# Attention block, batch of 32: TensorE's wait for the output weight moved into slot 4 of each batch, and a value copy moved ahead of an exponential on ScalarE

## The chip, the cores and the metric

The kernel runs on one core of one Trainium2 chip. The metric is the time of one execution on the device in microseconds, of which the median of several runs is given. Profiles are of one execution; their times are microseconds from the first instruction. A core has five engines that run their own instruction queues and meet at semaphores: TensorE (PE in the rows; PEld is its weight load), VectorE (DVE), ScalarE (ACT), GpSimd (POOL) and SyncE (SP), which here issues all DMAs.

## The reference

For each of 32 batches of 256 tokens and 512 features the kernel computes a normalisation, attention with 16 heads of 32 features and an additive bias, an output projection and a residual:

```python
h = jnp.maximum(_layernorm(x, axis=-1), 0.0)
q, k, v = split_heads(h @ Wq.T), split_heads(h @ Wk.T), split_heads(h @ Wv.T)
a = jnp.einsum('bhnd,bhmd->bhnm', q, k) * D ** (-0.5) + 2 * adj
row_nonzero = jnp.any(a != 0, axis=-1, keepdims=True)
p = softmax(a) where row_nonzero, else 0
o = jnp.einsum('bhnm,bhmd->bhnd', p, v).transpose(0, 2, 1, 3).reshape(B, N, D)
return x + o @ Wo.T
```

(The bias is the sum of two encodings that are both `adj`.)

## The kernel before

Each engine has a program of its own, with a prologue for the weights, then `body` for batch 0, a hardware loop over batches 1 to 30, and `body` for batch 31. `body` runs over 16 slots, one for each head `hh`. In slot `hh` TensorE transposes the probabilities of head `hh` (`transpose_probs`, L429), computes the scores of head `hh + 3` (`scores`, L415), in even slots the weighted values of heads `hh - 2` and `hh - 1` (`values`, L450 and L451), and then the slot's jobs from the table `JOBS`. A job is a part of a projection product or a group of transposes: `h` (normalised tokens turned), `qk`, `v` (value block `n`), `o` (attention output turned), `y` (output product). An entry is (kind, block, batch offset, first and last product). The slots that matter here are

```python
    2: [("v", 2, 0, 2, 12), ("v", 3, 0, 0, 3)],
    3: [("v", 3, 0, 3, 12), ("o", 1, -1, 0, 4)],
    4: [("h", 0, 1, 0, 4), ("y", 0, -1, 0, 6)],
    5: [("y", 0, -1, 6, 9), ("h", 1, 1, 0, 4), ("y", 0, -1, 9, 12)],
```

So slot 4 of batch b turns tokens of batch b + 1 and starts the output product of batch b - 1. Batch 0 has no jobs with offset -1, batch 31 none with offset 1.

Jobs write into two banks of PSUM in turn. Before a job starts, `begin` (L334) waits until the block that was last in its bank is taken. Taking a block is two steps: ScalarE copies the high part (`take`, L601), then VectorE computes the low part from the copy (`take`, L796) and signals `taken`. For `v` these are L622 and L818, for `o` L626 (oT_hi) and L822 (oT_lo), for `h` L610 and L804. The `y` job of slot 4 uses the bank of the `o` job of slot 3 and also reads oT_hi and oT_lo. Its waits, in order: the bank (`taken["o"]`, block 1), then at L394 `taken["o"]`, block 0.

ScalarE's slot (L692 to L712) is, in this order: in odd slots a copy of finished head outputs (L637); the exponential of head `hh + 1` (L648, two instructions); `take` of the jobs that ended in the slot before (`ended_before`), which for slot 4 are value block 3 and then o block 1; the copy of the high part of head `hh`'s transposes (L659). VectorE's slot (L910 to L926) is: the shift of head `hh + 2` (L843), its `take`s, the low part of head `hh`'s transposes (L852). Each engine works its queue in the order written.

GpSimd folds shifted scores (`fold`, L1050 and L1056), divides and scales head outputs (`divide`, L1017 to L1030; its result `o` is what the `o` jobs transpose), adds the residual (L1042), and in batch 0, in slots 7, 9, 11 and 13, computes the four low parts of the output weight (`low_out_weight`, L1063), each of which raises `wo_split` by one. The output weight's parts are read by `y` products only. TensorE waits for all four once, between `body(0, ...)` and the loop (L521).

Of the kernel before, what the change touches and what calls it, by code (L numbers as in the profile page):

```python
# [60 lines left out]
def jobs_at(hh, first, last):  # L61

    return [j for j in JOBS[hh] if not (first and j[2] < 0) and not (last and j[2] > 0)]


def ended_before(hh, first, last):

    if hh:
        return [j[:3] for j in jobs_at(hh - 1, first, last)
                if j[4] == PRODUCTS[j[0]]]  # L70
    return [(kind, n, d - 1) for kind, n, d, _, end in JOBS[HEADS - 1]
            if end == PRODUCTS[kind] and not (first and d < 1)]


def attention_block(nc, x, adj, wq, wk, wv, wo_t, out):
    B, N, D = x.shape
    NT = N // P
    KT = D // P
# [20 lines left out]
    with ExitStack() as ctx:  # L99
# [6 lines left out]
        def sem(name):  # L106
            return ctx.enter_context(nc.semaphore(name))
# [75 lines left out]
        wo_high, wo_split = sem("wo_high"), sem("wo_split")  # L183
# [40 lines left out]
        def bank(kind, n, b):  # L224


            if isinstance(b, int) and (kind, n, b) in OTHER_BANK:
                return 1 - BANK[kind, n]
            if isinstance(b, int) and (kind, n, b) == ("v", 0, 0):
                return 3  # L230
            return BANK[kind, n]

        def count(kind, n, b):

            return b * PER_BATCH[kind] + (n + 1)

        def head_no(b, hh):
            return b * HEADS + hh
# [91 lines left out]
        def _(pe):  # L330
# [23 lines left out]
            def job(kind, n, d, start, stop, b):  # L354
                ps = job_ps[bank(kind, n, b + d)]
                if start == 0:
                    begin(kind, n, d, b)
                if kind == "h":
                    if n == 0 and start == 0:

                        pe.wait_ge(h_ready, b + (d + 1))
                    for k, t in [divmod(i, NT) for i in range(start, stop)]:
                        end = nc.tensor.transpose(ps[:, k * N + t * P:k * N + (t + 1) * P],  # L363
                                                  h[:, t, (2 * n + k) * P:(2 * n + k + 1) * P], ident[:, :])
                elif kind == "qk":
                    half = PRODUCTS["qk"] // 2
                    if n == 0 and start == 0:

                        pe.wait_ge(taken["h"], count("h", 0, b + d))
                    if n == 0 and start <= half // 2 < stop:  # L370

                        pe.wait_ge(taken["h"], count("h", 1, b + d))
                    for i, w in enumerate((WQ, WK)):
                        if start < (i + 1) * half and stop > i * half:
                            end = product(ps[:, i * N:(i + 1) * N],
                                          [lambda k, w=m: w[:, k, n * P:(n + 1) * P] for m in (w_hi[w], w_lo[w])],
                                          [lambda k, v=v: v[:, k, :] for v in hT], start - i * half, stop - i * half)
                elif kind == "v":
                    t, half = n % NT, n // NT
                    end = product(ps[:, 0:HALF], [lambda k, v=v: v[:, k, t * P:(t + 1) * P] for v in hT],  # L380
                                  [lambda k, w=w: w[:, k, half * HALF:(half + 1) * HALF] for w in (w_hi[WV], w_lo[WV])],
                                  start, stop)
                elif kind == "o":

                    if start == 0:
                        pe.wait_ge(o_ready, (b + d) * QUADS + 2 * (n + 1))
                    for k, t in [divmod(i, NT) for i in range(start, stop)]:
                        end = nc.tensor.transpose(ps[:, k * N + t * P:k * N + (t + 1) * P],  # L388
                                                  o[:, t, (2 * n + k) * P:(2 * n + k + 1) * P], ident[:, :])
                else:  # L390
                    half = PRODUCTS["y"] // 2
                    if n == 0 and start == 0:

                        pe.wait_ge(taken["o"], count("o", 0, b + d))  # L394
                    if n == 0 and start <= half < stop:

                        pe.wait_ge(taken["o"], count("o", 1, b + d))
                    end = product(ps[:, :], [lambda k, v=v: v[:, k, n * P:(n + 1) * P] for v in oT],
                                  [lambda k, w=w: w[:, k, :] for w in (wo_hi, wo_lo)], start, stop)
                if stop == PRODUCTS[kind]:  # L400
                    end.then_inc(ended[kind], 1)
# [116 lines left out]

            body(0, True, False)

            pe.wait_ge(wo_split, KT)  # L521
            with pe.Fori(1, B - 1) as b:
                body(b, False, False)
            body(B - 1, False, True)
# [38 lines left out]
        def _(act):  # L563
# [37 lines left out]
            def take(kind, n, b, early=False):  # L601

                ps = job_ps[bank(kind, n, b)]
                if kind == "y" and not (isinstance(b, int) and b == 0):

                    act.wait_ge(stored[n], b * 16)

                act.wait_ge(ended[kind], count(kind, n, b))
                if kind == "h":
                    nc.scalar.activation(hT_hi[:, 2 * n:2 * n + 2, :], ps[:, :].rearrange("p (k n) -> p k n", k=2),  # L610
                                         ACT.Relu).then_inc(high["h"], 1)
                elif kind == "qk":
                    nc.scalar.activation(qk_parts[:, n // 2, 1, n % 2, :], ps[:, 0:N], ACT.Copy,
                                         scale=q_scale[:, n:n + 1])
                    nc.scalar.activation(qk_parts[:, n // 2, 2, n % 2, :], ps[:, N:2 * N], ACT.Copy,
                                         scale=UNTOP).then_inc(high["qk"], 1)
                elif kind == "v":
                    t, half = n % NT, n // NT
                    if not early:

                        act.wait_ge(pv_done, head_no(b, 0) + (HH * (half + 1) - HEADS))
                    nc.scalar.activation(v_parts[:, t, half * HH:(half + 1) * HH, 0:HD],  # L622
                                         ps[:, 0:HALF].rearrange("p (h d) -> p h d", d=HD), ACT.Copy,
                                         scale=V_UNTOP).then_inc(high["v"], 1)
                elif kind == "o":
                    nc.scalar.activation(oT_hi[:, 2 * n:2 * n + 2, :], ps[:, :].rearrange("p (k n) -> p k n", k=2),  # L626
                                         ACT.Copy).then_inc(high["o"], 1)
                else:
                    nc.scalar.activation(y[:, n, :], ps[:, :], ACT.Copy).then_inc(taken["y"], 1)

            def copy_outputs(b, pair, early):

                act.wait_ge(pv_done, head_no(b, 2 * pair + 2))
                if not early:

                    act.wait_ge(o_ready, b * QUADS + (pair // 2 - 1))
                nc.scalar.activation(o_raw[pair // 2 % 2][:, pair % 2, :, :],  # L637
                                     o_ps[:, :].rearrange("p (q c) -> p q c", c=P)[:, :, 0:LOW + HD],
                                     ACT.Copy).then_inc(o_copied, 1)
# [51 lines left out]
            def body(b, first, last):  # L691
                for hh in range(HEADS):  # L692
                    if hh % 2:

                        if hh > 1:
                            copy_outputs(b, hh // 2 - 1, first and hh < 10)
                        elif not first:
                            copy_outputs(b - 1, PAIRS - 1, False)
                    if hh + 1 < HEADS:
                        exponentials(b, hh + 1, first and hh + 1 < 2)  # L700
                    elif not last:
                        exponentials(b + 1, 0, False)
                    for kind, n, d in ended_before(hh, first, last):
                        take(kind, n, b + d, first and (kind, d) in (("v", 0), ("qk", 0)))
                    if first and 6 <= hh < 6 + KT:

                        high_out_weight(hh - 6)
                    if hh == HEADS - 3 and not (first or last):
                        copy_adj(b + 1)
                    high_probs(b, hh, first and hh < 4)  # L710
                    if hh == HEADS - 3 and first:
                        copy_adj(b + 1)  # L712
# [429 lines left out]
```

## Time and profile before

| | us |
|---|---|
| median of 3 runs | 1256.52 (1256.03 to 1256.82) |
| profiled execution, its own time | 1256.6 |
| its span, first to last instruction | 1254.8 |
| mean granted TensorE clock | 0.999 |

| engine | busy, us | share of span |
|---|---|---|
| TensorE, products | 1230.2 | 98% |
| TensorE, weight loads | 1109.2 | 88% |
| VectorE | 1068.7 | 85% |
| ScalarE | 1044.2 | 83% |
| GpSimd | 897.1 | 71% |

A busy share says how much of the span has an instruction recorded. Products are pipelined and the ends of their records are modelled, so two starts that are further apart than usual can be a wait though no idle time is recorded between them. A record that follows a wait carries in brackets the idle time before it and what released it.

### The profile page before, as it was taken

What the parts mean: (1) busy time and instruction counts of PE and PEld (TensorE: products, weight loads), DVE (VectorE), ACT (ScalarE), POOL (GpSimd) and SP (SyncE); (2) the same over time, 40 slices, a digit from 0 to 9 for tenths busy, and PEclk for the clock granted to TensorE, in tenths of its full rate; (3) what the DMA queues carried; (4) which work ended last, traced back from release to release, by engine and by line L of the source; (5) the groups of instructions that cost most, each with busy time, mean ns of one, the idle gap of its engine ahead of it and who ended that gap; (6) DMA issues with size and microseconds to landing.
All of it is one profiled execution on the core that took longest, in us unless ns stands there. A gap on an engine that the chain in (4) does not pass through costs nothing.

```text
span 1254.8 us, 43748 instructions
## 1 busy us (share of the span) xinstructions
PE 1230.2 (98%) x13104; PEld 1109.2 (88%) x13104; DVE 1068.7 (85%) x3500; ACT 1044.2 (83%) x2429; POOL 897.1 (71%) x1268
## 2 busy tenths in 40 slices
PE   6989999999999999999999999999999999999997
PEld 5878989989989999889989899899899898998996
DVE  7878888888888888888888888888888888888887
ACT  5878888888888888888888888888888888888886
POOL 4767776777776777777777776777767777767765
PEclk9999999999999999999999999999999999999999
DMA  6536445465445454454554454654454554545533
GB/s 228 127 101 151 116 111 141 117 159 137 122 109 136 131 150 131 118 127 123 145 150 117 113 138 116 159 139 120 109 138 130 150 133 117 126 125 143 134 97 89
DMA packets 91861, 163.89 MB, mean 131 GB/s; under 512 B 15168, under 2 KB 24896, under 8 KB 91840
## 3 DMA queue, kind: packets, MB, share of 16 engines
q1 hardware_dynamic: 91840, 163.64, 50.2%
q8 instruction: 10, 0.16, 0.1%
q14 instruction: 11, 0.09, 0.0%
HBM read 46.14 MB, written 16.78 MB: 50 GB/s over the span
## 4 chain that ended last, share of the span: by engine, by line
PE 88%; POOL 6%; issue 3%; DVE 1%; ACT 0%; DMA 0%; POOLq 0%; DVEq 0%; ACTq 0%
PE job_ps L348 51%; PE pT_ps L429 16%; PE s_ps L415 9%; PE o_ps L450 6%; PE o_ps L451 2%; POOL fold L1050 2%; PE job_ps L363 2%; PE job_ps L388 2%; POOL bounds L1056 1%; POOL o_raw L1024 1%; POOL o L1030 0%; POOL y L1042 0%; POOL wo_lo L1063 0%; DVE minus L843 0%; POOL h L1009 0%
## 5 line engine op out<-in xcount | busy, mean ns | idle before, releaser
L1050 POOL TENSOR_TENSOR fold<-minus 128x512 f32<-128x512 f32 x256 | 326.2, 1274 | 247.5 <-DVE bounds L843 247.4
L648 ACT ACTIVATE probs<-minus,bounds 128x256 f32<-128x256 f32 x1024 | 461.7, 503 | 10.8 <-DVE bounds L843 10.7
L852 DVE TENSOR_TENSOR pT_lo<-pT_ps,pT_hi 128x512 f16<-128x512 f32 x512 | 350.3, 684 | 124.8 <-ACT pT_hi L659 124.5
L843 DVE CUSTOM_DVE_ANT_0 minus<-s_ps,adj_now 128x256 f32<-128x256 f32 x1024 | 388.8, 417 | 13.1 <-issue 6.6
L659 ACT ACTIVATE pT_hi<-pT_ps 128x512 f16<-128x512 f32 x512 | 305.8, 597 | 111.2 <-PE pT_ps L429 109.5
L429 PE MATMUL pT_ps<-ident,probs 128*128 128x128 f32 x2048 | 308.1, 273 | 4.5 <-POOL wo_lo L1063 2.8
L348 PE MATMUL job_ps<-hT_hi,w_hi 128*128 128x256 f16 x1024 | 280.7, 274 | 1.3 <-DVE hT_lo L804 1.0
L348 PE MATMUL job_ps<-hT_hi,w_lo 128*128 128x256 f16 x1024 | 279.5, 273 | 0.0
L348 PE MATMUL job_ps<-hT_lo,w_hi 128*128 128x256 f16 x1024 | 279.4, 273 | 0.0
L429 PEld LDWEIGHTS pT_ps<-ident,probs 128*128 128x128 f32 x2048 | 242.2, 141 | 22.3 <-issue 3.3
L415 PE MATMUL s_ps<-qk_stack 96*128 96x256 f32 x1024 | 246.7, 322 | 0.5 <-DMA qk_stack<-qk_parts 0.4
L1056 POOL TENSOR_TENSOR bounds<-fold 128x256 f32<-128x256 f32 x256 | 187.6, 733 | 25.1 <-POOL fold L1050 9.6
L415 PEld LDWEIGHTS s_ps<-qk_stack 96*128 96x128 f32 x1024 | 154.7, 191 | 1.0 <-DMA qk_stack<-qk_parts 0.7
L450 PE MATMUL o_ps<-v_parts,pT_hi 128*128 128x65 f16 x2048 | 152.3, 192 | 1.2 <-DVE pT_lo L852 1.0
L451 PE MATMUL o_ps<-v_parts,pT_lo 128*128 128x33 f16 x2048 | 146.2, 178 | 0.0
L348 PE MATMUL job_ps<-w_hi,hT_hi 128*128 128x256 f16 x508 | 139.5, 275 | 1.9 <-DVE qk_parts L812 0.9
L348 PE MATMUL job_ps<-w_lo,hT_hi 128*128 128x256 f16 x508 | 138.4, 272 | 0.0
L348 PE MATMUL job_ps<-w_hi,hT_lo 128*128 128x256 f16 x508 | 138.3, 272 | 0.0
L450 PEld LDWEIGHTS o_ps<-v_parts,pT_hi 128*128 128x128 f16 x2048 | 122.4, 96 | 13.1 <-DVE pT_lo L852 1.8
L451 PEld LDWEIGHTS o_ps<-v_parts,pT_lo 128*128 128x128 f16 x2048 | 125.3, 96 | 0.0
L348 PEld LDWEIGHTS job_ps<-hT_hi,w_hi 128*128 128x128 f16 x1024 | 99.8, 97 | 16.5 <-DVE hT_lo L804 1.1
L348 PEld LDWEIGHTS job_ps<-hT_hi,w_lo 128*128 128x128 f16 x1024 | 100.1, 98 | 12.0
(96 smaller groups left out, 2191.2 us busy)
## 6 DMA issues: line engine op xcount, KB each, us to landing
qk_stack<-qk_parts SPq DMA_DIRECT2D x756, 128.0 KB, 2.3
x_in<-x SPq DMA_DIRECT2D x32, 512.0 KB, 4.8
x_res<-x SPq DMA_DIRECT2D x32, 512.0 KB, 3.6
out<-y SPq DMA_DIRECT2D x64, 256.0 KB, 2.1
adj_in<-adj SPq DMA_DIRECT2D x32, 256.0 KB, 4.7
qk_stack<-qk_parts SPq DMA_DIRECT2D x24, 64.0 KB, 2.0
w_in<-wq SPq DMA_DIRECT2D x2, 512.0 KB, 5.4
w_in<-wk SPq DMA_DIRECT2D x2, 512.0 KB, 6.6
```

The lines of the kernel that those rows point to most:

```text
L348: end = nc.tensor.matmul(dst, lhs[a](k), rhs[c](k), start=i == 0, stop=i == len(terms) - 1)
L363: end = nc.tensor.transpose(ps[:, k * N + t * P:k * N + (t + 1) * P], h[:, t, (2 * n + k) * P:(2 * n + k + 1) * P], ident[:, :])
L415: end = nc.tensor.matmul(s_ps[SCORE_BANK[hh]][:, t * N:(t + 1) * N], stack[:, 0, t * P:(t + 1) * P], stack[:, 1, :], start=True, stop=True)
L429: end = nc.tensor.transpose(pT_ps[hh % 2][:, m * N + t * P:m * N + (t + 1) * P], probs[hh % 2][:, t, m * P:(m + 1) * P], ident[:, :])
L450: nc.tensor.matmul(ps[:, 0:LOW + HD], hi, v[:, 0:LOW + HD], start=m == 0, stop=False)
L451: end = nc.tensor.matmul(ps[:, 0:HD + 1], lo, v[:, 0:HD + 1], start=False, stop=m == NT - 1)
L648: end = nc.scalar.activation(probs[hh % 2][:, t, :], minus[hh // 2 % 2][:, hh % 2, t, :], ACT.Exp, bias=bounds[:, hh // 2 % 4, 2 * (hh % 2 ...
L659: nc.scalar.activation(pT_hi[hh % 4][:, :, :], pT_ps[hh % 2][:, :].rearrange("p (m n) -> p m n", m=NT), ACT.Copy).then_inc(pT_high, 1)
L843: end = nc.vector.tensor_tensor_reduce(out=minus[pair % 2][:, hh % 2, t, :], in0=s_ps[SCORE_BANK[hh]][:, t * N:(t + 1) * N], in1=adj_now[: ...
L852: nc.vector.tensor_tensor(pT_lo[hh % 4][:, :, :], pT_ps[hh % 2][:, :].rearrange("p (m n) -> p m n", m=NT), pT_hi[hh % 4][:, :, :], ALU.sub ...
L1050: nc.gpsimd.tensor_tensor(f1[:, :, :], src[:, :, 0:N // 2], src[:, :, N // 2:N], ALU.add).then_inc(folded1, 1)
L1056: nc.gpsimd.tensor_tensor(f2, f1[:, :, 0:N // 4], f1[:, :, N // 4:N // 2], ALU.add).then_inc(folded2, 1)
```

## The change

The wait of TensorE for the four parts of the output weight is taken out between batch 0 and the loop, and put into `job` ahead of the first `y` product of block 0, which stands in slot 4 of batches 1 to 31. On ScalarE, in slot 4 of every batch, the `take` of value block 3 is called ahead of the exponential of head 5 and left out of the list behind it. No operation is added or removed otherwise.

```diff
@@ def job
                 else:
                     half = PRODUCTS["y"] // 2
+                    if n == 0 and start == 0:
+
+                        pe.wait_ge(wo_split, KT)
                     if n == 0 and start == 0:
 
                         pe.wait_ge(taken["o"], count("o", 0, b + d))
@@ block.tensor
             body(0, True, False)
 
-            pe.wait_ge(wo_split, KT)
             with pe.Fori(1, B - 1) as b:
@@ block.scalar, body
+                    if hh == 4:
+
+                        take("v", 3, b, first)
                     if hh + 1 < HEADS:
                         exponentials(b, hh + 1, first and hh + 1 < 2)
                     elif not last:
                         exponentials(b + 1, 0, False)
                     for kind, n, d in ended_before(hh, first, last):
+                        if (kind, n) == ("v", 3):
+                            continue
                         take(kind, n, b + d, first and (kind, d) in (("v", 0), ("qk", 0)))
```

## Rows read from the trace of the kernel before

**Rows 1.** The page, part 1: busy time, share of the span, instructions.

```profile
PE 1230.2 (98%) x13104; PEld 1109.2 (88%) x13104; DVE 1068.7 (85%) x3500; ACT 1044.2 (83%) x2429; POOL 897.1 (71%) x1268
```

**Rows 2.** Timeline, TensorE, end of batch 0, start of batch 1: start, duration, instruction, [idle before].

```profile
67.10 0.27 PE L348 MATMUL job_ps<-w_hi,hT_lo 128*128 128x256 f16 x1
70.17 0.65 PE L429 MATMUL pT_ps<-ident,probs 128*128 128x128 f32 x4 [2.80 <-POOL wo_lo L1063]
...
76.55 0.60 PE L429 MATMUL pT_ps<-ident,probs 128*128 128x128 f32 x4
```

**Rows 3.** Timeline, TensorE, first output product of slot 4, batches 1 and 30.

```profile
82.87 0.50 PE L348 MATMUL job_ps<-wo_hi,oT_hi 128*128 128x512 f32 x1
...
1187.00 0.50 PE L348 MATMUL job_ps<-wo_hi,oT_hi 128*128 128x512 f32 x1
```

**Rows 4.** Timeline, TensorE, slots 3 to 5 of batch 2.

```profile
118.75 0.27 PE L348 MATMUL job_ps<-w_hi,hT_lo 128*128 128x256 f16 x1
118.86 0.60 PE L388 MATMUL job_ps<-ident,o 128*128 128x128 f32 x4
...
120.43 0.63 PE L363 MATMUL job_ps<-ident,h 128*128 128x128 f32 x4
120.95 0.50 PE L348 MATMUL job_ps<-wo_hi,oT_hi 128*128 128x512 f32 x1
...
123.80 0.60 PE L363 MATMUL job_ps<-ident,h 128*128 128x128 f32 x4
124.16 0.48 PE L348 MATMUL job_ps<-wo_hi,oT_hi 128*128 128x512 f32 x1
```

**Rows 5.** Timeline, GpSimd, end of batch 0 and start of batch 1.

```profile
68.57 1.26 POOL L1063 TENSOR_TENSOR wo_lo<-wo_in,wo_hi 128x512 fp32r<-128x512 f32 x1
69.79 1.27 POOL L1050 TENSOR_TENSOR fold<-minus 128x512 f32<-128x512 f32 x1
71.14 0.74 POOL L1056 TENSOR_TENSOR bounds<-fold 128x256 f32<-128x256 f32 x1
```

**Rows 6.** Table of windows: length, busy by engine, granted clock, DMA share, GB/s.

```profile
40.00:47.00 7.00, 5.50 (x70) 4.88 (x69) 7.00 (x22) 6.90 (x17) 5.18 (x8) 1.00 0.89 205
...
72.00:73.00 1.00, 1.00 (x6) 0.71 (x5) 1.00 (x6) 0.83 (x3) 0.00 (x0) 0.50 0.00 0
```

**Rows 7.** Timeline, TensorE, starts of slots 0 and 2 of batch 2.

```profile
109.96 0.60 PE L429 MATMUL pT_ps<-ident,probs 128*128 128x128 f32 x4
...
114.62 0.60 PE L429 MATMUL pT_ps<-ident,probs 128*128 128x128 f32 x4
```

**Rows 8.** Timeline, ScalarE and VectorE, slot 15 of batch 0.

```profile
64.98 0.91 ACT L648 ACTIVATE probs<-minus,bounds 128x256 f32<-128x256 f32 x2
...
64.97 0.68 DVE L852 TENSOR_TENSOR pT_lo<-pT_ps,pT_hi 128x512 f16<-128x512 f32 x1
```

**Rows 9.** Timeline, GpSimd, slots 1 to 3 of batch 2.

```profile
112.78 1.27 POOL L1050 TENSOR_TENSOR fold<-minus 128x512 f32<-128x512 f32 x1 [0.88 <-DVE bounds L843]
...
116.18 0.62 POOL L1030 TENSOR_TENSOR o<-o_raw,factor 128x256 f32<-128x256 f32 x1
```

**Rows 10.** Timeline, VectorE and TensorE, slot 4 of batch 31, the last.

```profile
1224.04 0.69 DVE L822 TENSOR_TENSOR oT_lo<-job_ps,oT_hi 128x512 fp32r<-128x512 f32 x1
...
1224.79 0.51 PE L348 MATMUL job_ps<-wo_hi,oT_hi 128*128 128x512 f32 x1 [0.29 <-DVE oT_lo L822]
```

**Rows 11.** Timeline, ScalarE, slot 4 of batch 2.

```profile
118.31 0.90 ACT L648 ACTIVATE probs<-minus,bounds 128x256 f32<-128x256 f32 x2
119.10 0.37 ACT L622 ACTIVATE v_parts<-job_ps 128x256 f16<-128x256 f32 x1
119.49 0.60 ACT L626 ACTIVATE oT_hi<-job_ps 128x512 fp32r<-128x512 f32 x1
```

**Rows 12.** Timeline, VectorE, slot 4 of batch 2.

```profile
120.12 0.69 DVE L822 TENSOR_TENSOR oT_lo<-job_ps,oT_hi 128x512 fp32r<-128x512 f32 x1
```

**Rows 13.** Timeline, TensorE, a wait in slot 6 of batch 0.

```profile
46.31 0.27 PE L348 MATMUL job_ps<-hT_hi,w_hi 128*128 128x256 f16 x1 [0.99 <-DVE hT_lo L804]
```

## The prediction

> **What bounds the kernel now.** The page comes first: TensorE is busy for 98% of the span [rows 1], so whatever moves TensorE's next instruction moves the end. Next comes the timeline of TensorE at its longest wait behind the prologue. It shows one large hole, between the last product of batch 0 and the first transpose of batch 1, ended by GpSimd's wo_lo [rows 2]. Then come the starts of one instruction over all batches: the first output product of slot 4 starts at 82.87 in batch 1 and at 1187.00 in batch 30 [rows 3], so a batch takes (1187.00 - 82.87) / 29 = 38.07 us. Anything that is added once in each batch counts 31 times. Last comes slot 4 on all engines, where the second half of the change lies; its rows are named there.
>
> **Part one: the wait for wo_split.** It stands before batch 1, though the output weight is first read in slot 4 of batch 1. TensorE's last product of batch 0 starts at 67.10, and the next instruction could start 0.11 later (the step from the last value product to the o transposes, 118.75 to 118.86, [rows 4]), at 67.21. It starts at 70.17, just after the fourth wo_lo ends at 68.57 + 1.26 = 69.83 [rows 2, 5]. That is 2.96 us. Behind the hole TensorE runs at half its clock: granted 0.50 in 72 to 73 (1.2 GHz of 2.4) [rows 6]. Slots 0 and 1 take 76.55 - 70.17 = 6.38 us in batch 1 and 114.62 - 109.96 = 4.66 in batch 2 [rows 2, 7], so the slow clock costs 1.72. Both go if nothing else is late: 4.68 us.
>
> What is late next? The first transposes of batch 1 need head 0's exponential, which ended at 64.98 + 0.91 = 65.89, and the split of head 14, which ended at 64.97 + 0.68 = 65.65 [rows 8]. Neither holds at 67.21. GpSimd is behind by its backlog: its fold of batch 1's pair 0 ends its second step at 71.14 + 0.74 = 71.88 [rows 5], whatever TensorE does. Then it folds pair 1 and divides the last quad of batch 0, which takes from 112.78 to 116.18 + 0.62 = 116.80 in batch 2 [rows 9], 4.02 us; so o would be ready at 75.90. Its reader, the o transposes of slot 3, stands at 118.86 in batch 2 [rows 4], that is 8.90 behind the batch's start, and so at 67.21 + 8.90 = 76.11. GpSimd is just in time, by 0.2 us. The moved wait itself is long met when slot 4 comes, about 10.5 us (120.43 - 109.96, [rows 4, 7]) behind the start, against 69.83.
>
> The wait is now executed in each of 31 batches. It stands behind the wait for the bank (oT_lo of the o block before) and ahead of another wait for o. Behind it are queued the six y products and all that TensorE does later. Once met it costs only its passage. The trace of before doesn't show one alone; but in the last batch the product's record starts at 1224.79, 0.06 behind the end of oT_lo at 1224.04 + 0.69 = 1224.73 [rows 10], with one met wait passed in that time. So the bound is 0 to 0.06 each, 0 to 1.9 us in all. I take 0, since part of that 0.06 must be the signal's way. The Trainium skill speaks against this (Advanced Engine Details and Errata, Miscellaneous Facts): reading a semaphore from a sequencer takes 50 to 100 ns, by which 31 reads would be an estimate of 1.6 to 3.1 us; the 0.06 of the row speaks against the upper end.
>
> **Part two: ScalarE's order in slot 4.** Now ScalarE does, in this order: exponential of head 5 (118.31), copy of value block 3 (119.10), copy of the o transposes (oT_hi, 119.49), copy of head 4's transposes [rows 11]. The last product of value block 3 starts at 118.75 and lasts 0.27, so it ends at 119.02 [rows 4]. The copy of block 3 is therefore only 0.08 late as it is. Put ahead of the exponential, it makes ScalarE stand still until 119.02 plus the signal; with 0.03 for that (118.86 + 0.60 = 119.46 to the start of oT_hi at 119.49, [rows 4, 11]) it starts at 119.05. The exponential has been ready since 118.31 and is queued behind it.
>
> A ScalarE operation starts 0.11 before the recorded end of the one before (118.31 + 0.90 = 119.21 against 119.10). So the exponential starts at 119.05 + 0.37 - 0.11 = 119.31, and oT_hi 0.79 to 0.81 later (I take 0.80), near 120.12 instead of 119.49: 0.63 us later. VectorE starts oT_lo 0.03 behind oT_hi's end (119.49 + 0.60 = 120.09, start 120.12) and ends at 120.81 [rows 11, 12]; it comes 0.63 later too, with head 4's split queued behind it.
>
> Is oT_lo on TensorE's path? The first y product starts at 120.95, 0.14 behind oT_lo's end, and 0.52 behind the first h transpose at 120.43. The same pair in slot 5, with no wait between, takes 124.16 - 123.80 = 0.36 [rows 4]. So the y product already waits up to 0.16, and there is no cover. In the last batch, without h transposes, the profile names oT_lo as its releaser outright [rows 10]. If the release takes 0.06 as there, and 0.08 of the 0.14 is something else, the shift in TensorE is 0.55; if the 0.14 stays, 0.63. I take 0.60 for 30 batches and 0.63 for the last: 18.0 + 0.6 = 18.6 us. The bounds are 30 x 0.55 + 0.63 = 17.1 and 31 x 0.63 = 19.5.
>
> Does TensorE get it back in the batch? What it waits for later (copies of h, exponentials, scores) follows TensorE's own, equally late work or keeps its distance: ScalarE's delay behind TensorE is gone once it waits for the transposes of slot 5. What the earlier copy gives, the bank for the h transposes, is worth nothing: they start right behind the head products, and VectorE's half of the value block isn't earlier, because it is queued behind the shift of head 6.
>
> Batch 0 has no y in slot 4; there the moved copy delays head 4's copy and the h copies by at most the same 0.63. I take 0.2, with 0 and 0.6 as bounds.
>
> **Sum.** -4.68 + 18.6 + 0.2 = +14.1 us on the profiled execution's 1256.6 us (span 1254.8, so 1.8 around it): 1270.7. That execution lies 0.1 above the median of 1256.52, so 1270.6. With the bounds: 1256.5 - 4.7 + 17.1 = 1268.9 at the low end; 1256.5 - 3.0 (the hole goes, the slow clock stays) + 19.5 + 0.6 + 1.9 = 1275.5 at the high one.
>
> **Rivals.**
> - Faster. VectorE's or TensorE's queue has slack I don't see, so that a later oT_lo moves no product, and only part one remains: 1256.5 - 4.7 = 1251.8. For it: in batches 1 to 30 the profile puts no idle time of TensorE down to oT_lo. Against it: 0.52 against 0.36, and the last batch. It decides if the y product could start 0.6 us after oT_lo ended without being late, and no row shows such slack.
> - Partly absorbed. Half to two thirds of the 0.63 arrives, since a later wait of TensorE in the batch shrinks by the rest: 31 x 0.3 to 0.4 = 9.3 to 12.4, so 1261 to 1264. For it, small steps like the 0.16; against it, the period of 38.07 that is full of TensorE's own work [rows 1].
> - Part one gives nothing. GpSimd's backlog takes the place of the wait: its margin is 0.2 us, and a stall there could cost up to the hole and the slow clock again. Then 1256.5 + 18.6 + 0.2 = 1275.3.
> - The clock falls in every batch, because of the new wait of some 0.75 us. A fall costs 1.72, so 1270.6 + 31 x 1.72 = 1323.9. Against it, TensorE stood idle for 0.99 us ahead of 46.31 [rows 13], and 40 to 47 has a granted clock of 1.00 [rows 6]. The Trainium skill names this behaviour (TensorE: Matmul & The Clock Gate, HAM oscillation): a kernel in which TensorE idles briefly between groups of products can make the clock swing. By that rule the time would be this rival's; the trace, with the idle time and clock just told, disagrees for single gaps of this size.
>
> **How the numbers follow.** Forecast 0.76; only part one 0.09; partly absorbed 0.05; nothing from part one 0.07; clock falls 0.03. A difference of 0.2% (2.5 us) is about what a measurement of this kernel can tell from no change. Only the first rival is faster: 0.09. Within 0.2% lies none of the cases, and I leave 0.02 for a mixture, out of the absorbed case. Slower: 0.89. The range takes the forecast with its bounds and the stall of GpSimd, and reaches down to the upper edge of the absorbed case: 1264 to 1277. Outside are only part one, most of the absorbed case, and the clock.
>
> **What would show it.** In the profile after: no hole at 67 and no stretch of half clock behind it; batch 1's slot 4 about 4.7 us earlier than now, its y product at 82.87 - 4.7 + 0.6 = 78.8; in each slot 4 the copy of block 3 with an idle time of ScalarE of about 0.65 that ends with a product of TensorE; the exponential behind it; the first y product about 1.1 behind the first h transpose instead of 0.52, with its wait put down to oT_lo; a period of 38.67 instead of 38.07. The prediction is wrong if that step stays near 0.5, if the period grows by less than 0.5, or if TensorE meets a new wait between 67 and 77.

## The result and the profile after

The changed kernel takes 1273.36 us (median of 4 runs, 1272.59 to 1274.25) against 1256.67 for the kernel before, run with it. The ratio is 1.0132, with a 95% interval of 1.0118 to 1.0147: slower by 16.7 us. The profiled execution took 1274.25 us, with a span of 1272.4.

The page after, part 1:

```profile
PE 1234.2 (97%) x13104; PEld 1109.6 (87%) x13104; DVE 1070.6 (84%) x3500; ACT 1040.6 (82%) x2429; POOL 896.8 (70%) x1268
```

Three rows of the waits after (engine and line, what it waited for: us in total, times, longest):

```profile
DVE oT_lo L829 <- ACT oT_hi L628: 31.1, 62, 1.2
...
ACT v_parts L624 <- PE job_ps L348: 21.4, 35, 0.6
...
PE job_ps L348 <- DVE oT_lo L829: 16.2, 31, 0.9
```

The first two of them before:

```profile
DVE oT_lo L822 <- ACT oT_hi L626: 12.8, 31, 1.2
...
ACT v_parts L622 <- PE job_ps L348: 0.8, 3, 0.4
```

Each engine has as many instructions as before, and no busy time differs by more than 4.0 us from the one before [rows 1]. What is new is a chain of waits, one of each in a batch: ScalarE waits for the products of the value block (35 times instead of 3), VectorE for oT_hi (62 times instead of 31), TensorE for oT_lo (31 times). The last one stood at 0.29 us in one batch before [rows 10].

Slot 4 of batch 2 after, in the timelines of ScalarE, VectorE and TensorE (start, duration, instruction, idle time before it). The last line is the first output product of slot 4 in batch 30:

```profile
117.65 0.38 ACT L624 ACTIVATE v_parts<-job_ps 128x256 f16<-128x256 f32 x1 [0.64 <-PE job_ps L348]
117.93 0.90 ACT L650 ACTIVATE probs<-minus,bounds 128x256 f32<-128x256 f32 x2
118.73 0.58 ACT L628 ACTIVATE oT_hi<-job_ps 128x512 fp32r<-128x512 f32 x1
...
119.34 0.69 DVE L829 TENSOR_TENSOR oT_lo<-job_ps,oT_hi 128x512 fp32r<-128x512 f32 x1 [0.59 <-ACT oT_hi L628]
...
119.02 0.63 PE L363 MATMUL job_ps<-ident,h 128*128 128x128 f32 x4
120.16 0.50 PE L348 MATMUL job_ps<-wo_hi,oT_hi 128*128 128x512 f32 x1 [0.51 <-DVE oT_lo L829]
...
1203.99 0.50 PE L348 MATMUL job_ps<-wo_hi,oT_hi 128*128 128x512 f32 x1 [0.51 <-DVE oT_lo L829]
```

Against [rows 4, 11, 12]: ScalarE stands still for 0.64 us, the exponential follows the value block, and oT_hi starts 1.08 us behind the start of the block's copy (118.73 - 117.65) instead of 0.39 (119.49 - 119.10). The first output product stands 1.14 behind the first h transpose instead of 0.52, so 0.62 more. From batch 2 to batch 30 it moves by (1203.99 - 120.16) / 28 = 38.708 us per batch; before, by (1187.00 - 120.95) / 28 = 38.073 [rows 3, 4]. The difference, 0.635, times 31 is 19.7 us. The earlier copy gave nothing back: VectorE's half of the value block starts 0.69 ahead of the first h transpose after (118.33 and 119.02) and 0.70 before (119.73 and 120.43).

The start of batch 1 after, timeline of TensorE (slots 0, 2 and the o transposes of slot 3) and of GpSimd:

```profile
69.86 0.60 PE L432 MATMUL pT_ps<-ident,probs 128*128 128x128 f32 x4
...
74.52 0.60 PE L432 MATMUL pT_ps<-ident,probs 128*128 128x128 f32 x4
...
78.75 0.60 PE L388 MATMUL job_ps<-ident,o 128*128 128x128 f32 x4
...
77.89 0.62 POOL L1037 TENSOR_TENSOR o<-o_raw,factor 128x256 f32<-128x256 f32 x1
```

The hole is gone, and slots 0 and 1 take 4.66 us instead of 6.38 [rows 2, 7]. GpSimd's `o` is ready at 77.89 + 0.62 = 78.51, 0.24 ahead of its reader. Slot 0 starts at 69.86, though, not at 67.21: batch 0 ends 2.65 us later than it did. The account of the span is so: 69.86 - 70.17 = -0.31 up to batch 1, 4.66 - 6.38 = -1.72 for the clock, +19.7 for 31 batches, together +17.7 against the measured 1272.4 - 1254.8 = +17.6. For the same reason the first output product of batch 1 starts at 81.47 and not at the forecast 78.8.

### The profile page after: what moved, and what is told of

It is laid out like the page before. It is cut to its first block, busy times and chain, and to the rows that moved or that the text cites. A ratio compares the mean times of both kernels' runs of the same rounds, so it can differ in the third digit from the quotient of the medians.

```text
span 1272.4 us, 43778 instructions
## 1 busy us (share of the span) xinstructions
PE 1234.2 (97%) x13104; PEld 1109.6 (87%) x13104; DVE 1070.6 (84%) x3500; ACT 1040.6 (82%) x2429; POOL 896.8 (70%) x1268
## 4 chain that ended last, share of the span: by engine, by line
PE 84%; issue 5%; POOL 4%; DVE 3%; ACT 3%; DMA 1%; SPq 0%; ACTq 0%; POOLq 0%; DVEq 0%
PE job_ps L348 51%; PE pT_ps L432 15%; PE s_ps L418 8%; PE o_ps L453 5%; PE o_ps L454 2%; POOL fold L1057 2%; DVE oT_lo L829 2%; ACT oT_hi L628 1%; PE job_ps L363 1%; ACT probs L650 1%; PE job_ps L388 1%; POOL bounds L1063 0%; POOL o_raw L1031 0%; POOL o L1037 0%; POOL y L1049 0%
## 5 line engine op out<-in xcount | busy, mean ns | idle before, releaser
L432 PEld LDWEIGHTS pT_ps<-ident,probs 128*128 128x128 f32 x2048 | 242.2, 141 | 19.7 <-ACT probs L650 2.6
L348 PE MATMUL job_ps<-wo_hi,oT_hi 128*128 128x512 f32 x256 | 109.9, 429 | 16.5 <-DVE oT_lo L829 16.2
```

What stands on the lines that cost most here:

```text
L348: end = nc.tensor.matmul(dst, lhs[a](k), rhs[c](k), start=i == 0, stop=i == len(terms) - 1)
L432: end = nc.tensor.transpose(pT_ps[hh % 2][:, m * N + t * P:m * N + (t + 1) * P], probs[hh % 2][:, t, m * P:(m + 1) * P], ident[:, :])
```

## The experiments

### The wait's move alone

```diff
@@ block.scalar, body, against the changed kernel
-                    if hh == 4:
-
-                        take("v", 3, b, first)
@@
-                        if (kind, n) == ("v", 3):
-                            continue
```

> Only the move of TensorE's wait; ScalarE's order is that of before. Theory (the wait's hole and the slow clock behind it go, 2.96 + 1.72 us, the wait itself costs nothing): 1256.5 - 4.7 = 1251.8, period of a batch 38.07 as before, first y product of slot 4 still 0.52 behind the first h transpose. Rival 1 (the added wait delays each batch, up to 0.06 each): up to 1253.7. Rival 2 (part one gives nothing, since GpSimd's backlog takes the place of the wait): 1256.5, with a new idle time of TensorE between 67 and 77.

Measured: 1252.57 us (6 runs, 1251.57 to 1253.67), ratio to before 0.9968 (0.9955 to 0.9980). The first output product of slot 4 stands 0.51 behind the first h transpose (117.30 and 117.81), as before. So the first part of the change by itself is a gain of about 4 us. Rival 2 falls by the time, and TensorE has no new wait between 67 and 77. Rival 1 isn't excluded by the median, which lies inside its range; it falls by the unchanged step, and by the run with five waits below. The profiled execution of this kernel (1253.67 us) had a fall of the clock in batch 0, which is looked at below.

### ScalarE's order alone

```diff
@@ block.tensor, against the changed kernel
-                    if n == 0 and start == 0:
-
-                        pe.wait_ge(wo_split, KT)
@@
             body(0, True, False)
 
+            pe.wait_ge(wo_split, KT)
             with pe.Fori(1, B - 1) as b:
```

> Only ScalarE's order of slot 4; TensorE's wait stands before batch 1 as before. Theory (oT_hi, and with it the y product, 0.63 us later in each of 31 batches): 1256.5 + 19.5 = 1276.0, plus what batch 0 loses, 0.2 by the prediction and 2.6 by the profile of the changed kernel (slot 0 of batch 1 would start at 67.21 before and starts at 69.86 after): 1276.2 to 1278.6. Period 38.70. Rival (the two edits act together, the late y product is due to the wait that was put before it): 1256.5 and a period of 38.07.

Measured: 1276.59 us (1275.40 to 1277.27), ratio 1.0155 (1.0138 to 1.0172). Slot 4 of batch 5 takes 3.76 us against 3.15 before and 3.77 in the changed kernel, and TensorE's wait for oT_lo has the same row of waits as there (16.2 us, 31 times). The late product is due to ScalarE's order alone, not to the wait that was put before it.

### The new order from batch 1 on

```diff
@@ block.scalar, body, against the changed kernel
-                    if hh == 4:
+                    if hh == 4 and not first:
@@
-                        if (kind, n) == ("v", 3):
+                        if (kind, n) == ("v", 3) and not first:
```

> Both edits, but ScalarE's new order from batch 1 on only; batch 0 has the order of before. It tells whether the 2.6 us that the profile after shows over the sum in batch 0 come from the new order there. If so: 1256.5 - 4.7 + 19.5 = 1271.3, slot 7 of batch 0 at about 47.6 as before, no slow clock around 48 to 52. Rival (they come from how the DMAs of the prologue fell in that execution): like the changed kernel, 1273.4.

Measured: 1272.01 us (1271.13 to 1273.02), ratio 1.0119 (1.0102 to 1.0136). The time agrees with the theory within 0.7 us, but the reason does not hold as written. This kernel has the old order in batch 0, and its profile shows a slow clock there all the same (granted 0.50 in 47 to 50), so the new order isn't needed for it.

### Both copies ahead of the exponential

```diff
@@ block.scalar, body, against the changed kernel
                     if hh == 4:
 
                         take("v", 3, b, first)
+                        if not first:
+                            take("o", 1, b - 1)
@@
-                        if (kind, n) == ("v", 3):
+                        if (kind, n) in (("v", 3), ("o", 1)):
```

> Like the changed kernel, and from batch 1 on the copy of the o transposes (oT_hi) is put ahead of head 5's exponential too. ScalarE still stands still for value block 3, and the exponential comes another 0.5 us later. Theory (what costs is the exponential between the products' end and oT_hi): oT_hi starts at its old distance, 0.03 behind the o transposes' end, the y product 0.52 behind the first h transpose, period 38.07; total 1251.8 plus up to 2.6 for batch 0, 1251.8 to 1254.4. Rival (what costs is ScalarE's idle time ahead of value block 3, some 0.65 us in each batch, wherever it shows): 1271 or more, period 38.7 or more.

Measured: 1264.62 us (1263.79 to 1265.51), ratio 1.0064 (1.0048 to 1.0081): between the wait's move alone and the changed kernel, and outside the ranges of both the theory and the rival. Slots 4 and 5 of batch 2, timelines of ScalarE, VectorE and TensorE:

```profile
115.78 0.39 ACT L624 ACTIVATE v_parts<-job_ps 128x256 f16<-128x256 f32 x1 [0.65 <-PE job_ps L348]
116.21 0.60 ACT L628 ACTIVATE oT_hi<-job_ps 128x512 fp32r<-128x512 f32 x1
116.71 0.90 ACT L650 ACTIVATE probs<-minus,bounds 128x256 f32<-128x256 f32 x2
...
119.05 0.60 ACT L612 ACTIVATE hT_hi<-job_ps 128x512 f16<-128x512 f32 x1
...
120.13 0.64 DVE L813 SCALAR_TENSOR_TENSOR hT_lo<-job_ps,hT_hi 128x512 f16<-128x512 f32 x1
...
117.15 0.63 PE L363 MATMUL job_ps<-ident,h 128*128 128x128 f32 x4
117.67 0.50 PE L348 MATMUL job_ps<-wo_hi,oT_hi 128*128 128x512 f32 x1
...
120.83 0.66 PE L363 MATMUL job_ps<-ident,h 128*128 128x128 f32 x4
```

A row of the waits of this kernel (PEld is TensorE's weight load):

```profile
PEld job_ps L363 <- DVE hT_lo L813: 17.0, 30, 0.6
```

The theory holds for slot 4: the same idle time of ScalarE is there (0.65), and the output product is back at 0.52. So the idle time by itself costs nothing; what costs is the exponential between the products' end and oT_hi. But the total was wrong. ScalarE's work is now late behind the exponential, the h copy of slot 5 with it (119.05, that is 1.90 behind the first h transpose, where before it was 121.70 - 120.43 = 1.27), VectorE's low part (hT_lo) ends at 120.13 + 0.64 = 120.77, and the second h transposes, which need that bank, start at 120.83: 3.68 behind the first ones, where it was 3.37 before (123.80 - 120.43, [rows 4]). The row of waits names this releaser in 30 batches. With some hundredths more behind them slot 5 takes 2.88 us instead of 2.51 (both in batch 5). 30 batches x 0.37 = 11.1 us over the wait's move alone, plus 0.6 for batch 0, makes 1264.3. The cost had moved one slot on.

### The value block between the halves of the exponential

```diff
@@ block.scalar, against the changed kernel
-            def exponentials(b, hh, early):
+            def exponentials(b, hh, early, between=None):
...
                 for t in range(NT):
+                    if t and between is not None:
+                        between()
                     end = nc.scalar.activation(probs[hh % 2][:, t, :], minus[hh // 2 % 2][:, hh % 2, t, :], ACT.Exp,
...
-                    if hh == 4:
-
-                        take("v", 3, b, first)
                     if hh + 1 < HEADS:
-                        exponentials(b, hh + 1, first and hh + 1 < 2)
+                        exponentials(b, hh + 1, first and hh + 1 < 2,
+                                     (lambda: take("v", 3, b, first)) if hh == 4 else None)
```

> TensorE's wait moved as in the change; ScalarE takes value block 3 between the two halves of head 5's exponential, in every batch. Theory (every 0.1 us that oT_hi is late is 0.1 us on TensorE): first half at 118.31 by the times of batch 2 before, block 3 at 119.05 when its products have ended, second half at 119.31, oT_hi at 119.71 instead of 119.49, 0.22 late; 31 x 0.22 = 6.8 us over the move of the wait alone (1252.6): 1259.4, slot 4 takes 3.14 + 0.22 = 3.36 us. Rival (there is slack between oT_hi and the y product, so that a small delay is swallowed): 1252.6 and 3.14.

Measured: 1259.83 us (7 runs, 1258.94 to 1260.09), ratio 1.0027 (1.0016 to 1.0039). Slot 4 of batch 2, ScalarE and TensorE:

```profile
115.11 0.39 ACT L624 ACTIVATE v_parts<-job_ps 128x256 f16<-128x256 f32 x1 [0.25 <-PE job_ps L348]
115.39 0.50 ACT L652 ACTIVATE probs<-minus,bounds 128x256 f32<-128x256 f32 x1
115.79 0.59 ACT L628 ACTIVATE oT_hi<-job_ps 128x512 fp32r<-128x512 f32 x1
...
116.48 0.63 PE L363 MATMUL job_ps<-ident,h 128*128 128x128 f32 x4
117.23 0.50 PE L348 MATMUL job_ps<-wo_hi,oT_hi 128*128 128x512 f32 x1
```

The product stands 0.75 behind the first h transpose, 0.23 more than before, for a forecast of 0.22; slot 4 takes 3.37. Together with the kernels before and after this is a straight line: with oT_hi late by 0, 0.22 and 0.63 us (the forecasts), slot 4 takes 3.14, 3.37 and 3.77 us. So there is no slack between oT_hi and the output product.

### Five waits instead of one

```diff
@@ job, against the wait's move alone
                     if n == 0 and start == 0:
 
-                        pe.wait_ge(wo_split, KT)
+                        for _ in range(5):
+                            pe.wait_ge(wo_split, KT)
```

> The move of the wait alone, with the wait for wo_split written five times in a row ahead of the first y product, four more than the change has, all long met. ScalarE's order is that of before. Theory (a met wait is passed while the bank's wait holds or costs next to nothing): 1252.6 as with one, slot 4 takes 3.14. Rival (a met wait costs up to the 0.06 us that the prediction bounded it with): 31 x 4 x 0.06 = 7.4 us more, 1260.0, slot 4 takes 3.38. The page's 50 to 100 ns for one reading of a semaphore (the Trainium skill, Advanced Engine Details and Errata, Miscellaneous Facts) would give an estimate of 6.2 to 12.4 us more.

Measured: 1251.84 us (6 runs, 1251.26 to 1252.18), ratio 0.9967 (0.9954 to 0.9979), span 1250.1. Timeline of TensorE in batch 1: the starts of slots 0 and 4, the pair in slot 4, and the o transposes of slot 3; then GpSimd's `o` ahead of them; then VectorE and TensorE in slot 4 of batch 31:

```profile
67.21 0.60 PE L433 MATMUL pT_ps<-ident,probs 128*128 128x128 f32 x4
...
76.55 0.60 PE L433 MATMUL pT_ps<-ident,probs 128*128 128x128 f32 x4
77.69 0.63 PE L363 MATMUL job_ps<-ident,h 128*128 128x128 f32 x4
78.20 0.49 PE L348 MATMUL job_ps<-wo_hi,oT_hi 128*128 128x512 f32 x1
...
76.11 0.60 PE L388 MATMUL job_ps<-ident,o 128*128 128x128 f32 x4
...
75.26 0.62 POOL L1033 TENSOR_TENSOR o<-o_raw,factor 128x256 f32<-128x256 f32 x1
...
1219.36 0.69 DVE L825 TENSOR_TENSOR oT_lo<-job_ps,oT_hi 128x512 fp32r<-128x512 f32 x1
...
1220.11 0.51 PE L348 MATMUL job_ps<-wo_hi,oT_hi 128*128 128x512 f32 x1 [0.29 <-DVE oT_lo L825]
```

The step in slot 4 is 0.51 with five waits, and in batch 31 the product starts 0.06 behind the end of oT_lo (1220.11 - 1220.05), exactly as in the kernel before, which has none of them there [rows 10]. So a met wait costs nothing here, against the forecast's bound of 0.06. The 50 to 100 ns for one reading that the Trainium skill gives (Advanced Engine Details and Errata, Miscellaneous Facts) would have made an estimate of 6.2 us at least for four more in each of 31 batches, and no difference shows. All of these waits stand behind the bank's wait, which is still open when TensorE reaches them; whether a met wait is free elsewhere too isn't told by this run. The profile also has the first part of the prediction's sum in pure form: batch 1 starts at 67.21, and the first product of slot 4 moves from 82.87 [rows 3] to 78.20, by 4.67 us. GpSimd's `o` is ready at 75.26 + 0.62 = 75.88, and its reader starts at 76.11: the forecasts were 75.90 and 76.11.

### The new order in batch 0 alone

```diff
@@ block.scalar, body, against the changed kernel
-                    if hh == 4:
+                    if hh == 4 and first:
@@
-                        if (kind, n) == ("v", 3):
+                        if (kind, n) == ("v", 3) and first:
```

> The wait moved; ScalarE's new order in batch 0 alone. Theory (the order costs batch 0 some 0.64 us, of it 0.27 between slots 5 and 6 and 0.37 between slots 6 and 7 where the clock holds; the rest of what batch 0 lost in the changed kernel's profile was a fall of the clock in slots 6 and 7, which comes and goes between executions of any of these kernels): slot 5 of batch 0 takes 1.38 instead of 1.11, later batches 38.07, time 1252.6 + 0.6, give or take the 1.6 of the fall. Rival (the new order makes the clock fall): a fall here, and none in a kernel with the order of before; the profile of the move of the wait alone, with its granted clock of 0.50 in 47 to 50, speaks against it.

Measured: one run with its profile, 1252.3 us, span 1250.5. TensorE in batch 0, the starts of slots 5, 6 and 7 of this kernel, with a wait in slot 5 and one in slot 6:

```profile
41.90 0.60 PE L432 MATMUL pT_ps<-ident,probs 128*128 128x128 f32 x4
...
42.86 0.50 PE L418 MATMUL s_ps<-qk_stack 96*128 96x256 f32 x2 [0.37 <-DMA qk_stack<-qk_parts]
...
43.64 0.60 PE L432 MATMUL pT_ps<-ident,probs 128*128 128x128 f32 x4
...
46.86 0.27 PE L348 MATMUL job_ps<-hT_hi,w_hi 128*128 128x256 f16 x1 [0.99 <-DVE hT_lo L811]
48.17 0.60 PE L432 MATMUL pT_ps<-ident,probs 128*128 128x128 f32 x4
```

Slots 5 and 6 take 48.17 - 41.90 = 6.27 us; before, they took 47.62 - 41.97 = 5.65. So the order costs batch 0 0.62 us. In this execution all of it shows in slot 5 (1.74 instead of 1.12), behind a wait for a DMA, and isn't split over both slots as I had expected. In the profile of the order alone, where the clock held too, slots 5 and 6 took 1.38 and 4.90, together 6.28: the split differs, the sum doesn't. What sets the sum is VectorE, whose last low part of h the products of slot 6 wait for. Its split of head 4 and that low part, in the kernel before:

```profile
41.63 0.69 DVE L852 TENSOR_TENSOR pT_lo<-pT_ps,pT_hi 128x512 f16<-128x512 f32 x1
...
45.48 0.68 DVE L804 SCALAR_TENSOR_TENSOR hT_lo<-job_ps,hT_hi 128x512 f16<-128x512 f32 x1
```

And in this kernel:

```profile
42.18 0.69 DVE L859 TENSOR_TENSOR pT_lo<-pT_ps,pT_hi 128x512 f16<-128x512 f32 x1 [0.59 <-ACT pT_hi L661]
...
46.03 0.68 DVE L811 SCALAR_TENSOR_TENSOR hT_lo<-job_ps,hT_hi 128x512 f16<-128x512 f32 x1
```

The split waits for ScalarE's copy of head 4, which is late, and starts 0.28 behind the start of slot 5 (42.18 - 41.90) instead of 0.34 ahead of it (41.97 - 41.63). From there VectorE takes 3.85 us to the low part in both kernels, with no idle time between. The clock stayed up. The time is that of a single run, so it carries less than the profile.

The starts of slots 5, 6, 7 and 8 of batch 0 in the kernel before, timeline of TensorE:

```profile
41.97 0.60 PE L429 MATMUL pT_ps<-ident,probs 128*128 128x128 f32 x4
...
43.09 0.60 PE L429 MATMUL pT_ps<-ident,probs 128*128 128x128 f32 x4
...
47.62 0.60 PE L429 MATMUL pT_ps<-ident,probs 128*128 128x128 f32 x4
...
49.62 0.60 PE L429 MATMUL pT_ps<-ident,probs 128*128 128x128 f32 x4
```

The table of windows for 47 to 50 us (length, busy by engine, granted clock, DMA share, GB/s), in the kernel before:

```profile
47.00:50.00 3.00, 3.00 (x31) 2.78 (x28) 1.65 (x6) 2.28 (x6) 2.47 (x4) 1.00 0.12 27
```

The same window in the changed kernel:

```profile
47.00:50.00 3.00, 2.68 (x17) 2.43 (x18) 1.45 (x6) 1.51 (x4) 2.41 (x4) 0.69 0.20 46
```

The same window in the kernel with the wait's move alone:

```profile
47.00:50.00 3.00, 3.00 (x16) 2.47 (x15) 0.45 (x4) 1.13 (x4) 2.47 (x4) 0.50 0.10 23
```

And TensorE's timeline in that kernel, the starts of slots 6 and 8 of batch 0 and the wait of slot 6:

```profile
43.00 0.60 PE L432 MATMUL pT_ps<-ident,probs 128*128 128x128 f32 x4
...
46.23 0.27 PE L348 MATMUL job_ps<-hT_hi,w_hi 128*128 128x256 f16 x1 [0.99 <-DVE hT_lo L806]
...
51.18 0.60 PE L432 MATMUL pT_ps<-ident,probs 128*128 128x128 f32 x4
```

The wait's move alone has the work of the kernel before in batch 0, and the same wait of 0.99 in slot 6 [rows 13], and yet its clock was at half behind that wait. All nine profiles have this wait of 0.99. Slots 6 and 7 took 51.18 - 43.00 = 8.18 us there and 49.62 - 43.09 = 6.53 before: the fall cost 1.65. It was there in three of the profiles (the changed kernel, the wait's move alone, the new order from batch 1 on) and not in the six others (before, the order alone, both copies ahead, between the halves, five waits, the new order in batch 0 alone): old order and new one stand on either side. The shorter waits ahead of it don't tell them apart either: in slot 6 they were 0.27 and 0.25 us with the new order from batch 1 on, where the clock fell, and 0.28 and 0.23 with five waits, where it didn't. So the new order isn't what makes the clock fall; whether it makes a fall more likely is open, since each kernel has one profile, and so is what decides it.

## Why the prediction was right

It gave 1270.6 us in a range of 1264 to 1277; 1273.4 was measured. The mechanism was right. What was missed all lies on one side (too small), so no two errors cancelled to make the number look good. Step by step:

- **The wait's move, -4.68 us.** Right in both terms: 67.21 and -4.67 in the profile with five waits. GpSimd came just in time, as worked out (0.2 forecast, 0.23 with five waits and 0.24 in the changed kernel). The median of the wait's move alone moved by 4.2 us only, and with five waits by 4.3, so the profiles show the term more sharply than the medians, in which falls of the clock can be mixed.
- **The added wait, 0 us of 0 to 1.9.** Right. The 0.06 that I took for the bound isn't the wait's: it stands there with five waits too, so it is the way from oT_lo's end to the product.
- **The late oT_hi, 18.6 us.** The mechanism was right at each link: ScalarE's idle time forecast at 0.65 and measured at 0.64, the exponential behind the block, oT_lo as the named releaser. The size came out just above the upper bound of 19.5: I took 0.60 between 0.55 and 0.63, because I thought that 0.08 of the 0.14 between oT_lo's end and the product [rows 4, 12] might be something else. After, the distance is 120.16 - (119.34 + 0.69) = 0.13, so all of it belongs to the release, and a batch grew by 0.635. 31 x 0.635 = 19.7: mis-sized by 1.1 us.
- **Batch 0, 0.2 us of 0 to 0.6.** Too small: the order costs 0.62 there, just above the upper bound. I had costed it by what is delayed on ScalarE and not followed it through VectorE's full queue to the low part of h that TensorE waits for in slot 6. On top of that comes the fall of the clock, 1.65, in some executions.
- **The rivals.** Only part one, partly absorbed, nothing from part one: none of them came. The run with both copies ahead comes nearest to the absorbed case, with 0.37 lost in each batch, but by a loss one slot on and not by an absorption. The clock doesn't fall in every batch: the mean granted clock is 0.999 over the execution, with a wait of 0.51 to 0.9 us in each slot 4. But the row on which I based this, idle for 0.99 us with the clock at 1.00 [rows 6, 13], proves less than I made of it: with the same idle time in the same place the clock fell in another execution. What the prediction cites from the Trainium skill on brief idle times stands on that page (TensorE: Matmul & The Clock Gate) in the section A second HAM failure mode: psum-queue depth-cycling, one behind the section that it names.

The corrected sum, 1256.5 - 4.7 + 19.7 + 0.6 = 1272.1, lies 1.3 under the median. For the profiled execution the sum closes: with the fall of the clock (1.65), and with 0.35 by which slot 0 of batch 0 starts later (31.23 instead of 30.88), it is 1274.1 against 1274.25. With the 0.62 of the order, these are also the parts of the 2.65 us by which batch 0 ends later. Where the 0.35 come from is open. For the other three executions, 1272.6 to 1273.9, there is no profile; that falls of the clock fill their distance to the sum is likely by size, not shown.

## What to carry to other kernels

Before a copy is moved ahead on an in-order engine, look at when its input is ready: here the copy was only 0.08 us behind its input, so the move could hardly gain anything, and it put 0.64 us of waiting in front of an exponential that was ready and of everything behind it. Follow the queue past the moved instruction to the first result that another engine waits for, and look there for slack by comparing its step with the same step where there is no wait. A wait that guards data from a slow side computation belongs at the first use, even when it is then executed in every iteration, if a met wait costs as little as it did here. The part of this change to keep is the wait's move alone: it is 0.3% faster than the kernel before.

## What the runs showed of the hardware that was not expected

The clock's fall is not fixed by the work ahead of it: with the same idle time of 0.99 us ahead of slot 6's products, the granted clock behind it stayed at 1.00 in six profiles and was 0.50 (1.2 GHz) for about 3 us in three, which cost 1.65 us where it could be read. Four of these kernels have equal work in batch 0: before and five waits without a fall, the wait's move alone and the new order from batch 1 on with one. The Trainium skill (TensorE: Matmul & The Clock Gate, Part 1: The HAM clock gate) says that the number of slow products at the start of a kernel can differ between its runs. The falls here stand in the middle of batch 0, not at the start; that they too differ between executions of equal work agrees with it.

Five met waits in a row on TensorE's queue, behind a wait that was still open, took no time that the profile or the time shows (0.06 from oT_lo's end to the product with none of them and with five).
